# A graph network's scatter stage: how far a bucket's fields, tables and rows follow its last quad

## The reference, cut to what matters

```
x = ln(x + relu(segment_sum(h2[src, rel_type] * norm, dst) + bias2))      # layer 0
x = ln(x + elu(segment_sum(x[src] * a, dst)))   # layer 1, a: softmax of an edge weight by dst
x = ln(x + two rounds of segment_sum(w * x[c], r))                        # layer 2
gate = silu(edge_attr @ W1.T + b1) @ W2.T + b2 + adapt
msg = gate * h[dst] * (cw * mj)                                           # layer 3
x = ln(x + ln(h + segment_sum(msg, src) / tot) * gamma + beta)
```

## Time and profile before

| | us |
|---|---|
| runs of the kernel before | 6902.73, 6898.89, 6873.34 |
| median | 6898.89 |
| the profiled execution's own time | 6892.13 |
| its span, first to last instruction | 6890.3 |
| mean granted TensorE clock over the span | 0.605 |
| busy: VectorE, GpSimd, TensorE, ScalarE | 4075.6, 3960.8, 3922.0, 2567.7 |

### The profile page before, as it was taken

One profiled execution on the slowest core, in us unless ns is written; L12 is line 12 of the kernel. 1 busy time (PEld: TensorE's weight loads), 2 busy tenths in 40 slices (PEclk: granted clock), 3 DMA queues, 4 the chain that ended last, 5 costly groups with the idle time before them and its releaser, 6 DMA issues.

```text
span 6890.3 us, 121918 instructions
## 1 busy us (share of the span) xinstructions
PE 3922.0 (57%) x46612; PEld 3008.3 (44%) x46613; DVE 4075.6 (59%) x7184; ACT 2567.7 (37%) x5259; POOL 3960.8 (57%) x3993
## 2 busy tenths in 40 slices
PE   5445555555555554345555555555555555887875
PEld 5344444323323333134444444444444444776774
DVE  4444443555555556345666666566666558667999
ACT  1111111111111111244455455445445445776664
POOL 2566666666666666655555555555555553225996
PEclk8555555555555555555555555555555556999998
DMA  3444311121111121123333233333333332667886
GB/s 127 167 160 161 124 49 47 48 55 49 47 49 47 48 49 47 32 50 54 58 56 57 56 58 55 56 56 58 55 58 56 55 56 54 189 189 172 193 191 130
DMA packets 1414672, 571.31 MB, mean 83 GB/s; under 512 B 1069539, under 2 KB 1353711, under 8 KB 1413953
## 3 DMA queue, kind: packets, MB, share of 16 engines
q1 hardware_dynamic: 1309185, 452.39, 29.3%
q0 software_dynamic: 104896, 110.96, 6.7%
HBM read 394.81 MB, written 168.16 MB: 82 GB/s over the span
## 4 chain that ended last, share of the span: by engine, by line
another core or an unknown queue 22%; PE 19%; issue 18%; ACT 15%; DVE 14%; DMA 9%; SPq 2%; POOL 1%; DVEq 0%; ACTq 0%; POOLq 0%
DMA rb<-dst_rows 5%; PE ps L1247 4%; ACT rb L1603 3%; DMA meta_b<-blocks 3%; ACT at_table L1633 3%; ACT meta_b L1613 2%; DVE ps L2096 2%; ACT meta_a L1535 2%; PE ps L1285 2%; PE ps L1418 2%; PE ps L1207 2%; ACT meta_b L1620 1%; PE ps L1235 1%; PE ps L1295 1%
## 5 line engine op out<-in xcount | busy, mean ns | idle before, releaser
L925 POOL DMA_INDIRECT by_src<-meta_a,row_src x1612 | 1613.9, 1001 | 1336.6 <-DVE meta_a L2351 916.7
L914 POOL DMA_INDIRECT ring<-h_table,meta_b x1616 | 1646.1, 1019 | 941.0 <-issue 449.7
L1520 ACT ACTIVATE ring<-ring,meta_b 128x48 f32<-128x48 f32 x1616 | 387.7, 325 | 2144.7 <-DMA ring<-h_table,meta_b 2076.2
L1418 PE MATMUL ps<-dst_i,meta_b 128*128 128x128 bf16 x2450 | 395.8, 293 | 907.9 <-ACT at_table L1633 641.1
L1633 ACT ACTIVATE at_table<-ps 128x384 uint8<-128x384 f32 x817 | 397.6, 487 | 1276.3 <-remote 1126.7
L1247 PE MATMUL ps<-ring,WX 128*128 128x48 bf16 x2188 | 438.7, 235 | 542.5 <-DVE row_src L2227 308.9
L2589 DVE TENSOR_TENSOR meta_b<-big,ps 128x1152 bf16<-128x1152 bf16 x546 | 734.7, 1346 | 0.0
L1418 PEld LDWEIGHTS ps<-dst_i,meta_b 128*128 128x128 bf16 x2450 | 229.2, 151 | 1137.2 <-issue 1107.4
L1247 PE MATMUL ps<-row_src,WX 128*128 128x48 bf16 x4376 | 494.5, 233 | 253.6 <-issue 252.5
L1377 PE MATMUL ps<-WX,meta_b 128*128 128x49 bf16 (+1 forms) x14742 | 588.9, 200 | 66.9 <-issue 36.4
L1247 PEld LDWEIGHTS ps<-ring,WX 128*128 128x128 bf16 x2188 | 360.2, 165 | 572.1 <-DVE row_src L2227 317.9
(11 more groups left out here) (342 smaller groups left out, 8836.7 us busy)
## 6 DMA issues: line engine op xcount, KB each, us to landing
meta_b<-blocks SPq DMA_DIRECT2D x490, 144.0 KB
by_src<-default SPq DMA_DIRECT2D x44, 1456.0 KB
meta_a<-by_src SPq DMA_DIRECT2D x273, 216.0 KB, 4.4
rb<-lo_rows SPq DMA_DIRECT2D x202, 256.0 KB
rb<-src_rows SPq DMA_DIRECT2D x273, 144.0 KB
rb<-dst_rows SPq DMA_DIRECT2D x273, 144.0 KB
blocks<-at_table SPq DMA_DIRECT2D x229, 144.0 KB
meta_a<-in_attrT SPq DMA_DIRECT2D x402, 80.0 KB
```

The costliest lines, as they stand in the source:

```text
L914: pool.indirect_dma_start(ring[:, gg % RING, j, 0:width], None, table, bass.IndirectOffsetOnAxis(ap=index(g * GROUP + j), axis=0)) \
L925: pool.indirect_dma_start(by_src, bass.IndirectOffsetOnAxis(ap=row_src[:, t:t + 1], axis=0), rec[:, q % RECS, j, :], None).then_inc(s_sc[q ...
L1418: mm = pe.matmul(bank(5, P, at=i * P), ohS_n[:, a % 3, :, u * TRIO + i], ohK_n[:, a % 2, u * TRIO + i, :], start=True, stop=True)
```

## The change

The three lags become shorter: the fields, tables and rows of a bucket follow its last quad by 5, 7 and 9 quads. ROWS_LAG also sets where the steps stand, so STEP_AT, PLACES, BEHIND and AFTER follow. Nothing else is edited.

```diff
         NORM_AT = 7
-        FIELDS_LAG, TABLES_LAG, ROWS_LAG = 10, 13, 16
+        FIELDS_LAG, TABLES_LAG, ROWS_LAG = 5, 7, 9
```

## The result

The changed kernel takes 6918.23 us (median of 14 runs, 6900.44 to 6939.63); the kernel before, run beside it, 6900.5 us (median of 14, 6873.34 to 6911.08). The ratio is 1.0035, 95% interval 1.0023 to 1.0046: some 18 us slower by the medians and 24 by the ratio, where I had forecast 20 us faster. It stays within the 0.5% that I had called hard to tell, but these runs tell it from no change.

The account below looks back on a forecast made before the run. The scatter stage was taken as a chain of hand-overs with no engine full. Terms -23.9 + 10.1 + 5 - 31 + 20 = -20 us gave 6879 us against a median of 6898.89; range 6840 to 6938 us.

Parts of the forecast that it names:

- The end, -23.9 us: After the last quad's gates: 23 steps remain instead of 28, five fewer at 4.77 us each.
- Seven more quads with steps, +10.1 us: Middle of the scatter stage: seven more quads run at 7.36 us instead of 5.91; bounds 0 and 21 us.
- The front, +5 us: Bucket 0's fields hold up quad 18's attributes in SyncE's queue, so ScalarE's hidden sums come later; bounds 0 and 22 us.
- Nothing before its data, 0 us: Shorter distances from scatter to fields, table and rows still suffice (20.8, 17.0, 0.5 us); costed at nothing.
- The fields in the new place, +20 us: Fields behind two steps delay attributes in SyncE's queue: 13 buckets, 1.5 us each unhidden; bounds 0 and 48 us.
- The old place, -31 us: Attributes' lateness behind fields in stretches without steps goes away: half of 17 x 3.72 us; bounds 0 and 63 us.
- The first: Rival, among the steps: lateness paid in full, TensorE's clock falls too; 6993 us at most; chance 0.2.
- The second rival: Fields' old place was the bad one, the new costs nothing: 6822 us, or 6860 with part; chance 0.25.
- The third: Rival: shorter lags become waits, SyncE for tables or VectorE for fields; 6952 us; chance 0.1.
- the pace: Sign of error: time per quad among the steps differs from 7.36 us by over 0.1.
- The one on TensorE's idle time before L1285: Sign of error: TensorE's idle time before that line grows by half.
- No greater in sum: Profile forecast: TensorE's waits for attributes move from the stretch without steps to the fields' new place, their sum not growing.

Follow-up runs that it names:

- A: Condition of run sets in which the unchanged kernel takes about 6900 us; TensorE's granted clock over the stage is 0.56.
- B: Condition of run sets in which the unchanged kernel takes about 5610 us; TensorE's granted clock over the stage is 0.66.
- three scatters: One of each quad's four scatters left out, measured in A: kernel before 6467.36 us, with the change 6516.20, with the change and attributes one place earlier 6433.83.
- e1_order: Kernel before with lags of fields, tables and rows 12, 14, 16 instead of 10, 13, 16; steps and rows unmoved: ratio 1.0109 in B.
- e3_even: The change with every bucket's fields issued at an even place (lag 4 or 5): ratio 1.0009 to the kernel before, in B.
- b_before: The kernel before, unchanged, run again for its profile in B: ratio 1.0011 against itself.
- e2_shift: Kernel before with lags 3, 6, 9 instead of 10, 13, 16: all 7 places earlier, order and distances kept; ratio 1.0421 in B.

## Why the prediction was wrong

**The end, -23.9 us: right.** -26.8 in A, -25.8 in B, -27.2 with three scatters.

**Seven more quads with steps, +10.1 us: about right.** These are quads 26 to 33. From the gates of one to those of the other it took 41.4 us before and 48.7 after (2943.98 to 2992.66), +7.3. With three scatters it is +3.0 (32.9 to 35.9); in B the quads are faster after the stall at the front, and it does not show.

**The front, +5 us: nothing in A.** TensorE did stand 25.3 us for quad 18's attributes, behind bucket 0's fields. But from the gates of quad 17 to those of quad 26 it took 68.9 us before (2879.21 to 2948.09) and 69.3 after (2874.66 to 2943.98): the front's other work hid it. In B the same stall and a second one, for bucket 1, are not hidden: 21.9 us up to quad 26, of which 13.2 are left at quad 33, more than the term.

**Nothing before its data, 0 us: right at these lags in A, apart from the front.** No wait at L791, 21 us at L2301. Two places nearer it does cost, in B.

**The fields in the new place, +20 us: this step failed.** I had counted 13 of 45 buckets, those with fields at an odd place right behind two steps, at 3.7 us each, of which 2.2 were hidden. What the runs showed in its place:
- *How many.* The 13 were the right ones: TensorE waits in 13 of 13. What I had left out are the 15 buckets with fields at an even place behind two steps, where attributes two places on come late in 10: 32.2 us, 17.6 more than before at these places.
- *How long.* 97.5 us in the 13, 7.5 each and not 3.7. Bucket 4 shows why: SyncE gets to the fields at 3101.81, and TensorE is ready for the attributes at 3109.31. Into these 7.5 us I had put the issues alone, 10.25 us, and 1.0 us of landing. But the whole landing comes on top, 2.73 us here (3112.70 to 3115.43), and the issues took 10.79: together with the gaps 13.62 us, 6.12 over.
- *How much is hidden.* I had set TensorE's work in hand against the wait. The work in hand stands behind the wait in TensorE's order. In B the order alone (e1_order) raised TensorE's waits by 56.3 us and the gates' span by 62.1: nothing of this growth was hidden. (The sum is a coarse measure: e3_even has 82 us more of waits than b_before and loses 5 us.) With the shift, which has its own costs in the span, waits grew by 81.1 us in A and the span by 65.2; with three scatters by 94.2 and 76.4; in B by 130.9 and 86.7.
- *What it is worth.* From the old place to the new I had a net of -31 + 20 = -11 us. e1_order, which makes this move (and moves the tables by one place) but shifts nothing, lost 62 us in B. Attributes early against as before, at lags 5, 7, 9, give 98.6 us of gates' span in B and 85.7 with three scatters in A; with the old order in B they give 24.0. I had 20 at the likeliest and 48 at most for the new place.

**The old place, -31 us: not confirmed.** In B the edit that takes its lateness away gives 24 us of the gates' span and loses 18 at the end (17 and 20 when it was run again). In A it is not known by itself. The waits at that place did go, as forecast; they came back, and longer, two and three places on.

**Rivals.** The first had the sign and half the mechanism: lateness paid nearly in full, but no clock. The middle stayed at 0.56 with 81 us more of waits. I had set a rule of the Trainium skill ("TensorE: Matmul & The Clock Gate", section "HAM oscillation — how this bites in real kernels") beside it, by which waits between bursts of matmuls put the array back to half rate each time. By that rule the time would have been near 6950. The trace does not show it: 0.56 before and after. The second rival is refuted. The third named waits of VectorE for fields and of SyncE for tables; in B the first are there at the front and nowhere else of any size, and two places nearer it is SyncE's wait for scatters that costs (e2_shift). Of the signs of error that I had named, the pace was met: 7.52 us a quad from quad 33 (gates at 2992.66) to 402, for 7.36. The one on TensorE's idle time before L1285 was set too high to see it: all of it grew from 353.4 to 431.4 us, by 22%, the waits for attributes alone by 42%, neither by half. "No greater in sum" was the sharper statement, and it was wrong.

**Open.** Why the change costs 0.35% in A with four scatters and 0.75% (48.8 of 6467) with three. The waits' growth follows the pace: +81 us at 7.3 us a quad (gates' span of the kernel before over 402), +94 at 6.2, +131 at 5.3, as it should where 10.25 us of issues must fit between steps; but that is three points and no test. And in A with all four scatters neither the order by itself nor attributes early was run: there the cause is carried over from B and from the three-scatter set, and seen in the waits of after.

## What to carry to other kernels

When work moves in a queue, price what stands behind it, and not only what it waits for: find the transfer with the least time to spare, and count every place at which it follows, the next ones too. Before you set "work in hand" against a wait, read in the waiting engine's own order whether that work stands ahead of the wait or behind it. Count the landing as a whole against the time that is left, not only what it grows by. And try whether a queue's just-in-time transfers can be issued a place earlier in the buffers that they have: here, in B, that gave next to nothing with the old order (0.9985 and 0.9999) and made the shift pay (0.9927 and 0.9944, where the shift alone lost 1.1%).

## What was not expected of the hardware

**One kernel, two times.** 6900 and 5610 us. VectorE's, GpSimd's and ScalarE's busy times are the same within 0.5% (4075.6, 3960.8 and 2567.7 us in before, 4057.2, 3949.4 and 2565.2 in b_before), and a matmul of L1418 has a median of 311 ns in both. TensorE's granted clock over the stage differs, 0.56 and 0.66, and so does its busy time, 3922.0 and 3607.8 us. And an engine goes on sooner after another. First the kernel before in A, then in B: three matmuls of TensorE, and ScalarE's copy of their result:

```profile
4000.06 0.51 PE L1418 MATMUL ps<-dst_i,meta_b 128*128 128x128 bf16 x3 [3.11 <-issue]
...
4003.01 0.49 ACT L1633 ACTIVATE at_table<-ps 128x384 uint8<-128x384 f32 x1 [1.96 <-remote]
```

```profile
3203.25 0.39 PE L1418 MATMUL ps<-dst_i,meta_b 128*128 128x128 bf16 x3 [1.73 <-DVE meta_b L2589]
...
3203.68 0.49 ACT L1633 ACTIVATE at_table<-ps 128x384 uint8<-128x384 f32 x1 [1.33 <-PE ps L1418]
```

The copy starts 2.44 us after the recorded end of the matmuls (4000.57) in A, 0.04 us after it (3203.64) in B. Over all copies before which ScalarE was idle the median is 2.45 us in A and 0.04 in B; ScalarE's waits before L1633 sum to 1276 us in A (1126.7 of them "remote") and 450 in B. Not everything behind TensorE is late: ScalarE takes up the hidden sums (L1534) 0.04 us after L1286's recorded end in both. Whether the signals of these matmuls come late or they end later than recorded, whether the clock is part of the cause, and why it happens on one occasion and not on another (one chip number had both), was not found.

**A scatter less.** In A GpSimd waits 917 us for gates, and I had read that as "not the bound". Leaving out one scatter of four, 403 of about 1.0 us each, took 423 us off the kernel (6890 to 6467), where I had forecast 0.96 to 0.985, as much as if scatters were nothing but bound, while GpSimd's waits stayed near 1000 us. How the others get faster by it is open.

**A small transfer with a long issue.** Of the fields' four DMAs the two small ones are long in the queue: L783 moves 2.0 KB and takes 3.19 us, L786 1.0 KB and 6.79 us, each behind a large one (98 KB and 49 KB) that takes 0.34 us. The Trainium skill ("Perfetto Trace Analysis", section "DMA Instruction — HWDGE (DVE, Sync)") says that the profile's window of such an issue includes the wait for the unit that makes descriptors, and also the making of its own. The trace agrees with the first part in so far as the long issue is always the one behind the large transfer (L783 has a median of 3.32 us and L786 of 6.06 in after, L782 0.38 and L785 0.33). It does not fit the second, since the large transfers themselves show 0.3 to 0.4 us. That the 3 and 6 us belong to the large transfer ahead of each is argued from this, not shown: no run here changed their order or their pieces.
